# One-core transformer block, second attention: one update product over keys and negated keys, first normalisation on ScalarE

## The reference, cut to what matters

```python
sq = _sigma(q)                                   # elu + 1
denom_q = jnp.sum(sq * z[:, :, None, :], axis=-1, keepdims=True) + EPS
A_mem = jnp.matmul(sq, M) / denom_q              # what the queries read
scores = ...                                     # causal within the segment
A_dot = jnp.matmul(jax.nn.softmax(scores, axis=-1), v)
A_s = beta * A_mem + (1.0 - beta) * A_dot
sk = _sigma(k)
denom_k = jnp.sum(sk * z[:, :, None, :], axis=-1, keepdims=True) + EPS
V_prev = jnp.matmul(sk, M) / denom_k             # what the keys read
M_new = M + jnp.einsum('bhtk,bhtv->bhkv', sk, v - V_prev)
z_new = z + jnp.sum(sk, axis=-2)
```

## Time and profile before

| | |
|---|---|
| median of 3 runs | 1734.57 us (1734.44 to 1736.59) |
| the profiled execution | 1733.57 us |
| its span in the profile | 1731.8 us |
| PE busy | 1501.8 us (87%) |
| DVE busy | 1354.8 us (78%) |
| ACT busy | 813.1 us (47%) |
| POOL busy | 880.2 us (51%) |
| mean granted clock of TensorE | 0.949 |

### The profile page before, as it was taken

The page is one execution under the profiler, slowest core; times in us unless marked ns, Lnnn a source line. Parts: engine busy times, 40 slices in busy tenths (PEclk is TensorE's granted clock), DMA queues, the critical chain, the costliest instruction groups (busy, mean ns, idle before and its releaser), DMA issues. The chain is left out here.

```text
span 1731.8 us, 46136 instructions
## 1 busy us (share of the span) xinstructions
PE 1501.8 (87%) x13668; PEld 1285.4 (74%) x13668; DVE 1354.8 (78%) x3426; ACT 813.1 (47%) x1859; POOL 880.2 (51%) x1180
## 2 busy tenths in 40 slices
PE   5999999999999999996687648888888888888887
PEld 4999898998898998995566436666666666666665
DVE  5589999999999999995345366788887877788874
ACT  1556666665665666664466523333333333333331
POOL 4365565665566665654688543333343433333331
PEclk9999999999999999998799868999999999999997
DMA  4432233322222322220444232333333333333330
GB/s 141 142 94 89 78 82 91 91 81 74 81 82 91 91 76 76 80 76 15 136 124 132 58 93 86 96 99 100 98 102 97 101 97 100 98 101 100 94 92 17
DMA packets 181694, 158.10 MB, mean 91 GB/s; under 512 B 12529, under 2 KB 163185, under 8 KB 181618
## 3 DMA queue, kind: packets, MB, share of 16 engines
q1 hardware_dynamic: 181618, 157.17, 31.3%
HBM read 113.09 MB, written 44.04 MB: 91 GB/s over the span
## 5 line engine op out<-in xcount | busy, mean ns | idle before, releaser
L587 PE MATMUL a_bank<-a_vp,a_prob 128*128 128x96 f32 x4096 | 635.2, 261 | 0.0
L587 PEld LDWEIGHTS a_bank<-a_vp,a_prob 128*128 128x128 f32 x4096 | 610.7, 192 | 5.6
L481 ACT ACTIVATE a_prob<-a_bank 128x512 f32<-128x512 f32 x512 | 305.9, 598 | 267.9 <-PE a_bank L571 267.0
L675 DVE TENSOR_REDUCE a_nmax<-a_bank 128x2 f32<-128x512 f32 x512 | 345.1, 680 | 47.7 <-PE a_bank L556 40.7
L556 PE MATMUL a_bank<-a_k_st,a_q_st 96*128 96x256 bf16 x1024 | 259.2, 276 | 36.3 <-DVE a_nmax L675 35.1
L571 PE MATMUL a_bank<-a_q_st,a_k_st 120*128 120x256 bf16 x1024 | 281.7, 276 | 3.2 <-POOL a_q_st L344 3.2
L1613 PE MATMUL c_o_bank<-c_vb,c_prob 128*128 128x96 f32 x1024 | 176.6, 297 | 30.1 <-DVE c_ad L1896 29.3
L344 POOL TENSOR_SCALAR a_q_st<-a_mt 24x2048 bf16<-24x2048 bf16 x64 | 121.4, 1896 | 138.9 <-PE a_bank L571 94.8
L1771 DVE TENSOR_REDUCE c_nmax<-c_bank 128x4 f32<-128x512 f32 x256 | 165.0, 681 | 31.4 <-PE c_bank L1583 29.9
L1487 ACT ACTIVATE c_prob<-c_bank 128x256 f32<-128x256 f32 x256 | 98.8, 386 | 176.2 <-PE c_bank L1563 174.5
L1613 PEld LDWEIGHTS c_o_bank<-c_vb,c_prob 128*128 128x128 f32 x1024 | 141.1, 199 | 41.4 <-DVE c_ad L1896 29.1
(11 more groups left out here) (202 smaller groups left out, 2999.8 us busy)
## 6 DMA issues: line engine op xcount, KB each, us to landing
a_q_st<-scratch_a_parts_dram SPq DMA_DIRECT2D x64, 288.0 KB
a_k_st<-scratch_a_parts_dram SPq DMA_DIRECT2D x192, 96.0 KB
c_q_st<-scratch_c_parts_dram SPq DMA_DIRECT2D x64, 288.0 KB
c_k_st<-scratch_c_parts_dram SPq DMA_DIRECT2D x192, 96.0 KB
scratch_a_parts_dram<-a_parts SPq DMA_DIRECT2D x32, 384.0 KB, 2.7
scratch_c_parts_dram<-c_parts SPq DMA_DIRECT2D x32, 384.0 KB, 2.7
a_x<-in_x SPq DMA_DIRECT2D x32, 128.0 KB, 3.2
scratch_y<-a_y SPq DMA_DIRECT2D x32, 128.0 KB, 2.7
```

The source lines that it names most:

```text
L481: act.activation(prob[h % 4][:, :, :].rearrange("p a b -> p (a b)"), t_ps[h % 2][:, :], ACT.Exp).then_inc(exped, 1)
L587: mm = pe.matmul(o_ps[g % 2][:, at:at + VC], prob[h % 4][:, c, t * P:(t + 1) * P], vp[o][:, c, :], start=c == 0, stop=c == NT - 1)
L675: dve.tensor_reduce(nmax[:, t, 2 * g:2 * g + 2], s_ps[t][:, :].rearrange("p (h k) -> p h k", h=2), AX.X, ALU.max, negate=True).then_inc(ma ...
```

## The change

Three edits in `attention_b`. (1) ScalarE, after copying keys to `skn` rows 0 to 63, also writes the negated keys of segments 1 and 2 to rows 64 to 127. `read` no longer subtracts: for c < 2 it multiplies the keys' rows of `ps_c` by the reciprocal straight into `uv` rows 64 to 127, and then the queries' rows into `am`; for c = 2 only the latter. The product of line 1642 then gives keys times values minus keys times reads in one go. It now waits for both. (2) The first normalisation, z, goes from VectorE's step 7 to ScalarE's step 6, as scale and bias; GpSimd makes the bias (`negm`, `shift`) in two more instructions. (3) The rest of VectorE's order stays, and waits on counters are renumbered.

```diff
--- before.py
+++ after.py
@@ -1190,6 +1190,7 @@
         z, zt = two("z", [P, NT, P]), two("zt", [P, NS, 2, SEG])
         stats, mv = two("stats", [P, NT, 6]), two("mv", [P, NT, 2])
         var, rs = two("var", [P, NT]), two("rs", [P, NT])
+        negm, shift = sb("negm", [P, NT]), sb("shift", [P, NT])
         kq = two("kq", [P, 2, T])
         rest = sb("rest", [P, 2, T])
         parts = two("parts", [P, 2, NPART, T], BF16)
@@ -1272,7 +1273,7 @@
         x_dram, out_dram, wc_dram = pairs(d["x2"]), pairs(d["out"]), d["folded"]
         parts_dram = d["c_parts_dram"]
         flat = lambda a: a[:, :, :].rearrange("p c f -> p (c f)")
-        N_LOAD, N_LATE, SPLIT, MP, AD, VD = 3, 4, 4, 8, 6, 4
+        N_LOAD, N_LATE, SPLIT, MP, AD, VD, NORM = 3, 4, 4, 8, 6, 4, 4
         MT_AT = (3, 7)
 
         def value_part(a, t, p):
@@ -1389,6 +1390,14 @@
                 pool.wait_ge(mv_d[k], (b + 1) * NT)
                 apart(pool, spare)
                 pool.tensor_scalar(var[k][:, :], mv[k][:, :, 1], EPS, 1.0, ALU.add, ALU.mult).then_inc(norm_d[k], 1)
+                if k == 0:
+                    pool.tensor_scalar(negm[:, :], mv[0][:, :, 0], -1.0, 1.0, ALU.mult, ALU.mult
+                                       ).then_inc(norm_d[0], 1)
+                    pool.wait_ge(norm_d[0], NORM * b + 2)
+                    pool.tensor_tensor(rs[0][:, :], var[0][:, :], half[:, :], ALU.pow).then_inc(norm_d[0], 1)
+                    pool.wait_ge(norm_d[0], NORM * b + 3)
+                    pool.tensor_tensor(shift[:, :], negm[:, :], rs[0][:, :], ALU.mult).then_inc(norm_d[0], 1)
+                    return
                 pool.wait_ge(norm_d[k], 2 * b + 1)
                 pool.tensor_tensor(rs[k][:, :], var[k][:, :], half[:, :], ALU.pow).then_inc(norm_d[k], 1)
 
@@ -1492,6 +1501,8 @@
                             act.wait_ge(mem_p, b * 3)
                         act.copy(skn[0:SEG, :, :].rearrange("p s f -> p (s f)"),
                                  ps_c[0:SEG, 0:(NS - 1) * P]).then_inc(sk_d, 1)
+                        act.mul(skn[SEG:P, 1:NS - 1, :].rearrange("p s f -> p (s f)"),
+                                ps_c[0:SEG, P:(NS - 1) * P], -1.0).then_inc(sk_d, 1)
                     if s == 0 and active(j, u, 3):
                         b = n - 3
                         act.wait_ge(at_p, b + 1)
@@ -1528,6 +1539,13 @@
                             b = n - 1
                             act.wait_ge(mt_p, 2 * b + h2 + 1)
                             act.copy(late[h2][SEG:BROWS, :], mt_ps).then_inc(mt_d, 1)
+                    if s == 6 and active(j, u, -1):
+                        act.wait_ge(norm_d[0], NORM * (n + 2))
+                        if later(j, n, 1):
+                            act.wait_ge(zt_p, n)
+                        for t in range(NT):
+                            act.activation(z[1 - i][:, t, :], x[1 - i][:, t, :], ACT.Identity,
+                                           scale=rs[0][:, t:t + 1], bias=shift[:, t:t + 1]).then_inc(z_d, 1)
                     if s == 5 and active(j, u, 3):
                         b = n - 3
                         act.wait_ge(z4_p, b + 1)
@@ -1635,10 +1653,11 @@
 
                         b, c = n - 1, s // 2
                         if c == 0:
-                            pe.wait_ge(sk_d, b + 1)
+                            pe.wait_ge(sk_d, 2 * (b + 1))
                             pe.wait_ge(vs_d, b + 1)
                         else:
                             pe.wait_ge(u_d, b * 2 + c)
+                            pe.wait_ge(read_d, b * 9 + 3 * c)
                         pe.matmul(ps_c[:, 0:MW], skn[:, c, :], uv[o][:, c, :], start=True, stop=True
                                   ).then_inc(mem_p, 1)
                     if s in (2, 4, 6) and active(j, u, 1):
@@ -1801,12 +1820,14 @@
                     elif k == 1:
                         dve.reciprocal(dr[:, c, :], dn[:, c, :]).then_inc(read_d, 1)
                     elif k == 2:
-                        dve.tensor_tensor(by_head(am[o][:, c, :]), by_head(ps_c[:, 0:HV]),
-                                          dr[:, c, :].unsqueeze(2).broadcast_to([P, H, HD]), ALU.mult
+                        if c < 2:
+                            dve.tensor_tensor(by_head(uv[o][SEG:P, c + 1, 0:HV]),
+                                              by_head(ps_c[0:SEG, 0:HV]),
+                                              dr[0:SEG, c, :].unsqueeze(2).broadcast_to([SEG, H, HD]), ALU.mult
+                                              ).then_inc(u_d, 1)
+                        dve.tensor_tensor(by_head(am[o][SEG:P, c, :]), by_head(ps_c[SEG:P, 0:HV]),
+                                          dr[SEG:P, c, :].unsqueeze(2).broadcast_to([SEG, H, HD]), ALU.mult
                                           ).then_inc(read_d, 1)
-                    elif c < 2:
-                        dve.tensor_tensor(uv[o][0:SEG, c + 1, 0:HV], uv[o][0:SEG, c + 1, 0:HV],
-                                          am[o][0:SEG, c, :], ALU.subtract).then_inc(u_d, 1)
 
                 if isinstance(j, int) and n == 0:
                     stack_zeros(0)
@@ -1837,15 +1858,16 @@
                         for k in range(2):
                             remember(s // 2, k)
                     if s == 4 and active(j, u, 1):
-                        for k in range(4):
+                        for k in range(3):
                             read(1, k)
                     if s == 6 and active(j, u, 1):
 
                         for k in range(4):
                             split_max(1, k)
-                            read(2, k)
+                            if k < 3:
+                                read(2, k)
                     if s == 2 and active(j, u, 1):
-                        for k in range(4):
+                        for k in range(3):
                             read(0, k)
                     if s == 2 and active(j, u, 3):
 
@@ -1873,10 +1895,6 @@
                         if later(j, b, 2):
                             dve.wait_ge(x4_out, (b - 1) * 16)
                         dve.tensor_tensor(flat(x4[o]), ps_b[:, 0:T], flat(xb[o]), ALU.add).then_inc(x4_d, 1)
-                    if s == 7 and active(j, u, -1):
-                        if later(j, n, 1):
-                            dve.wait_ge(zt_p, n)
-                        normed(0, n + 1, x[o], z[o], z_d)
                     if s == 7 and active(j, u, 2):
 
                         b = n - 2
```

More of the change, by code:

```diff
@@ L1455, in body @@
                 if isinstance(j, int) and -1 <= n < 1:
-                    pool.wait_ge(norm_d[0], 2 * (n + 2))
+                    pool.wait_ge(norm_d[0], NORM * (n + 2))
                     value_consts(n + 1)
@@ L1827, in body @@
                         if later(j, n, 0):
-                            dve.wait_ge(norm_d[0], 2 * (n + 1))
+                            dve.wait_ge(norm_d[0], NORM * (n + 1))
                         moments(0, n + 1, x[o])
```

## The result

The changed kernel takes 1694.84 us, the median of 4 runs (1690.28 to 1697.76), against 1734.63 before: a ratio of 0.977, with a 95% interval of 0.974 to 0.979. The forecast was 1684 with a range of 1674 to 1704. The direction and the main mechanism held; the gain is 39.8 us where 50 were forecast. The profiled execution is the longest of the four; its span is 1696.0 us, 35.8 less than before.

The account below looks back on a forecast made before the run. TensorE sets the pace, VectorE second, with waits and low clock costing time. Terms 37.4 + 2 + 12 - 1.0 = 50.4 us off 1733.57 gave 1683, as a median 1684; range 1674 to 1704.

Parts of the forecast that it names:

- the main mechanism: In the read, removing VectorE's subtraction of two SBUF inputs ends its standing behind GpSimd and TensorE's low clock: 37.4 us.
- The hold goes and the clock stays up: At line 1808's subtraction: excess beside GpSimd's line 1427 and TensorE's low clock afterwards both vanish, 37.4 us.
- The rival of a clock that falls anyway: TensorE's remaining waits at lines 1642 and 1613 still lower its clock: 19 us of the sum lost, 1703; chance 0.11.
- A product with one PSUM input is not held: In the read, VectorE's product replacing the subtraction does not stand still beside GpSimd's instruction: zero excess in all 32 blocks.
- 13 of 32 blocks: In the read before the change, blocks where VectorE's subtraction started ahead of GpSimd's line 1427; used for the slower rival, 1748.
- Edit 2 gives 0.41 us a body: At the body's end, without z on VectorE, line 1892 and TensorE start 0.41 us earlier: 29 x 0.41 = 12 us.
- The cover on ScalarE and GpSimd: Negated copy, at most 0.4 us, and z work hide in these engines' idle time; only 1.0 us once at stage start.
- The pair takes 0.24 + 0.29 = 0.53, 0.07 less: In the read at c = 0 and 1, two products replace `am` and subtraction; counted once per block, 2 us.
- At c = 2 nothing changes but the row count: In the read at c = 2, VectorE's product only covers fewer rows; no time gained or lost was counted.
- the 2 us: In the read, gain from the two VectorE products being quicker than `am` plus subtraction: 32 x 0.07.
- counted c = 1 as free: In the read at c = 1, TensorE comes later than VectorE, so the 0.07 us gain counts only once per block.
- its 12: At the body's end, the gain from moving z off VectorE: 29 x 0.41 = 12 us, bounds 0 and 17.

Follow-up runs that it names:

- The twins: Changed kernel with second product on 128 rows plus an extra VectorE instruction at c = 0: two SBUF inputs, 1736.71 us; one PSUM input, 1689.76 us.
- the twin: Changed kernel with second product on 128 rows plus an extra VectorE instruction at c = 0 with one PSUM input: 1689.76 us, ratio 0.974 to before.
- edit 1 alone: Changed kernel with z back on VectorE in step 7 and without GpSimd's two extra instructions: 1711.70 us, ratio 0.987 to before.
- With 128 rows: Changed kernel with the second product of each read covering all 128 rows, not rows 64 to 127: 1681.53 us, again 1678.07 us.
- alone, edit 2: Changed kernel with the subtraction and 128-row `am` back and no negated copy, z still on ScalarE: 1739.99 us, ratio 1.003 to before.

## Why the prediction was right, and where it was off

*The hold goes and the clock stays up:* right, and the main term. Before, the 28 bodies to 1663.7 us took 33.5 us beyond 20.28 each; none is left. The twins show that the kind of input decides. The rival of a clock that falls anyway did not come true in the changed kernel.

*A product with one PSUM input is not held:* right, none of 96, and none of 32 in the twin. (The prediction gives VectorE 13 of 32 blocks before; one block has no split beside it, so it was 12 of 31.)

*Edit 2 gives 0.41 us a body:* right in place, a little small; the gap went from 0.98 to 0.50, and edit 1 alone differs from both edits by 0.48. The cover on ScalarE and GpSimd was there as costed.

*"The pair takes 0.24 + 0.29 = 0.53, 0.07 less", and "At c = 2 nothing changes but the row count":* this is the step that failed. It took 0.24, a mean over four products of which one step changes halves, as the price of every neighbour, and did not ask what the follower of the second product sees. Where neither has to wait for the other, the neighbours stand 0.21 us apart if they begin at the same partition and 0.30 to 0.33 if not. The pair changes halves, so it took 0.32 + 0.29 = 0.61 us, and TensorE's wait is 0.78 us as before (0.77): nothing of the 2 us came. The changed `am` begins at 64 and its follower at 0, so VectorE runs 0.117 us later behind it at each of c = 0, 1 and 2. TensorE waits for the sum of line 1879 behind c = 0 and for the sum of `mz` behind c = 1. The prediction counted c = 1 as free because the update product does not wait there; what follows on VectorE is waited for all the same.

That is 0.31 us a body, 10 us in all, nearly the whole gap of 10.8 us between forecast and median. That the rest closes so well is in part luck: the 2 us of the pair that did not come and the 2 us that edit 2 gave above its 12 cancel. With 128 rows the body is 19.82 us, where 19.8 was forecast, and the median 1678 to 1682, where 1684 was.

*That edit 2 is worth 12 us by itself* was never claimed, but the sum treats the edits as independent. They are not: alone, edit 2 costs 4 us (1739.99 against 1735.87 beside it).

## What to carry to other kernels

Look at the longest duration of a group beside its median: one instruction that sometimes takes four times as long, and a neighbour on GpSimd that starts hundredths of a microsecond ahead of it, is a hold whose price can be paid again in TensorE's clock. Here, giving VectorE's instruction a PSUM input ended it, from 0.07 us ahead of GpSimd's instruction to 0.31 us behind it. When rows of an instruction are cut to what is needed, ask where they begin: it can be dearer than computing all 128.

## What was not expected of the hardware

VectorE started an instruction 0.21 us behind one of 0.28 to 0.29 us where both begin at the same partition and neither waits for the other, and 0.30 to 0.33 us behind it, after its end, where they don't: 0.208 against 0.325 (median) for the follower of `am`; 0.208 against 0.316 for the two products of a read, where only the first one's output begins elsewhere. Partitions 0 and 64 are the only two compared.

A change that takes 0.6 us of work off VectorE made the kernel slower by 0.3% (0.2 to 0.4), because it turned 19 held instructions into 31.

Single low-clock stretches came in two kernels in which nothing was held, 6.8 us at 1286.7 and 3.4 us at 1353.8. Their cause is open, and so is why bodies with about the same waits keep the clock.
